# An mLSTM block with two MLPs on one core: the first block's weight split is moved beside the second block's tiles, its units run two at a time, and the gates' weights take 8 passes

## The reference

```python
h_in = rmsnorm(x, norm1_w)
q, k, v, o_pre = h_in @ wq, h_in @ wk, h_in @ wv, h_in @ w_og     # 8 heads
i_pre, f_pre = softcap(h_in @ w_ig + b_ig), softcap(h_in @ w_fg + b_fg)
Fcum = cumsum(log_sigmoid(f_pre))
Dmat = Fcum[:, None] - Fcum[None, :] + i_pre[None, :]; m = max(causal(Dmat))
C = (q @ k.T / sqrt(dqk)) * exp(Dmat - m)
h = (C / max(abs(sum(C)), exp(-m))) @ v
x1 = x + (sigmoid(o_pre) * headnorm(h)) @ w_out
h2 = rmsnorm(x1, norm2_w)
block = x1 + silu(h2 @ w_gate) * (h2 @ w_up) @ w_down              # FF = 2048
ghost = silu(x @ lut[gate_idx].T) * (x @ lut[up_idx].T) @ lut[down_idx].T   # 1376 inner
```

## Time and profile before

| | us |
|---|---|
| median of 3 runs | 2609.22 (2608.56 to 2611.22) |
| the profiled execution, its own time | 2609.44 |
| its span, first to last instruction | 2607.3 |

### The profile page before, as it was taken

The page is one execution under the profiler, slowest core; times in us unless marked ns, Lnnn a source line. Parts: engine busy times, 40 slices in busy tenths (PEclk is TensorE's granted clock), DMA queues, the critical chain, the costliest instruction groups (busy, mean ns, idle before and its releaser), DMA issues. The chain is left out here.

```text
span 2607.3 us, 32285 instructions
## 1 busy us (share of the span) xinstructions
PE 2458.7 (94%) x11024; PEld 1986.6 (76%) x11024; DVE 1270.9 (49%) x2185; ACT 914.5 (35%) x1667; POOL 605.7 (23%) x498
## 2 busy tenths in 40 slices
PE   6565999999999999999999999989999999999998
PEld 5344787877777777787777777768888888888887
DVE  5552563577477467557746746754322222222222
ACT  5313212444445353544444535346211111111111
POOL 4532221222122122222213212222111111111111
PEclk9568999999999999999999999999999999999999
DMA  5534645246445544724644554476687678767865
GB/s 219 205 142 148 243 154 198 98 157 234 158 148 190 205 144 161 290 96 159 230 161 143 198 202 145 160 285 224 220 288 272 242 261 290 256 239 278 284 213 199
DMA packets 117333, 530.32 MB, mean 203 GB/s; under 512 B 11280, under 2 KB 11280, under 8 KB 80304
## 3 DMA queue, kind: packets, MB, share of 16 engines
q1 hardware_dynamic: 110544, 515.86, 55.9%
q10 hardware_dynamic: 6624, 12.32, 1.6%
HBM read 440.46 MB, written 87.69 MB: 203 GB/s over the span
## 5 line engine op out<-in xcount | busy, mean ns | idle before, releaser
L1814 POOL TENSOR_TENSOR hidden_lo<-hm,hidden_hi 128x512 fp32r<-128x512 f32 x216 | 287.4, 1331 | 1360.7 <-ACT hidden_hi L972 1360.7
L664 PE MATMUL gate_bank<-act_hi,gud 128*128 128x512 f32 x1728 | 580.2, 397 | 17.1 <-DMA gud<-mlp_parts 9.0
L664 PE MATMUL up_bank<-act_hi,gud 128*128 128x512 f32 x1728 | 591.9, 404 | 0.0
L664 PE MATMUL acc<-gud,hidden_hi 128*128 128x512 f32 x1728 | 541.2, 395 | 16.8 <-POOL hidden_lo L1814 16.8
L1384 DVE SCALAR_TENSOR_TENSOR th<-th,gate_bank 128x512 f32<-128x512 f32 x216 | 147.9, 685 | 516.2 <-ACT th L967 516.2
L664 PEld LDWEIGHTS gate_bank<-act_hi,gud 128*128 128x128 f32 x1728 | 326.5, 189 | 85.4 <-issue 17.9
L664 PEld LDWEIGHTS up_bank<-act_hi,gud 128*128 128x128 f32 x1728 | 324.9, 188 | 79.2 <-issue 13.5
L664 PEld LDWEIGHTS acc<-gud,hidden_hi 128*128 128x128 f32 x1728 | 318.6, 188 | 83.4 <-issue 12.2
L972 ACT ACTIVATE hidden_hi<-hm 128x512 fp32r<-128x512 f32 x216 | 135.9, 629 | 697.9 <-PE acc L664 694.8
L664 PE MATMUL gate_bank<-act_lo,gud 128*128 128x512 f32 x864 | 338.2, 391 | 0.0
L664 PE MATMUL acc<-gud,hidden_lo 128*128 128x512 f32 x864 | 337.6, 391 | 0.0
(11 more groups left out here) (243 smaller groups left out, 3009.1 us busy)
## 6 DMA issues: line engine op xcount, KB each, us to landing
gud<-mlp_parts SPq DMA_DIRECT2D x128, 1024.0 KB, 5.1
gud<-ghost_parts SPq DMA_DIRECT2D x88, 1024.0 KB, 5.7
gud<-mlp_parts SPq DMA_DIRECT2D x128, 512.0 KB, 3.8
gud<-ghost_parts SPq DMA_DIRECT2D x88, 512.0 KB, 4.6
mlp_parts<-gud SPq DMA_DIRECT2D x16, 1536.0 KB, 6.0
ghost_parts<-look_w SPq DMA_DIRECT2D x35, 512.0 KB, 4.2
vo_w_hi<-vo_parts SPq DMA_DIRECT2D x12, 1024.0 KB, 5.9
vo_w_lo<-vo_parts SPq DMA_DIRECT2D x12, 1024.0 KB, 9.8
```

Source lines behind the costliest of these rows:

```text
L664: mm = pe.matmul(dst, l[a], r[c], start=first and k == 0 and n == 0, stop=last and k == len(lhs) - 1 and n == 2)
L1814: pool.tensor_tensor(HH[1][:], hm[:], HH[0][:].bitcast(f32), ALU.subtract).then_inc(of.low.sem, 1)
```

## The change

It does five things.

1. *Split.* Nothing of `mlp_parts` is made in FIRST. Tiles 0 and 1 are split in SECOND's front, tiles 2 to 15 in step t of `tiles(SECOND)`, gate and up parts in step t - 1, the down part in step t. PE uses the split tile from `gud` directly. A raw buffer of four tiles lies over the v/o weights, which are stored before and reloaded after (`reload_vo`, 4 MB). ACT's 128x1536 copy becomes one of 128x1024 and one of 128x512; POOL's three subtractions stay.
2. *Units.* FIRST's odd units get banks ACC[0], ACC[1] and buffers of their own. unit_1(u + 1) is put ahead of unit_2(u) on PE and DVE. x_T(FIRST), the second block's layer norm and the copy of its rows move into the units; the last ho_T, out-projections, x1 and h2 of FIRST move into SECOND's front.
3. *Gates.* High and low gate weights stand side by side as 32 columns: 8 passes instead of 12; two small DVE operations add the two halves.
4. *Block end.* x_T uses four banks, x_T(0) to x_T(3) all stand ahead of down(14), and down(15) moves behind the next front's gates. The wait for `mlp_rows` moves from DVE's first step of the front to ACT's row copy and to DVE's `cum`.
5. *Smaller moves.* In step 10 product(10) comes ahead of h2_scale(2). In TAIL the first index load is issued before the tiles, and bit_0 follows product(0) instead of preceding gated(0).

The core of the diff follows: the step counter, then SP, PE, ACT and DVE.

```diff
+class FirstAhead(Steps):
+    def of(self, at, k, name):
+        if not isinstance(at[0], int) or at != (0, 0):
+            return Steps.of(self, at, k, name)
+        i, n, e = self.names.index(name), len(self.names), self.early
+        if i < e:
+            return self.credit + i + 1 + (e + (k - 1) * n if k else 0)
+        return self.credit + e + k * n + (e if k + 1 < self.per_pass else 0) + i - e + 1
...
+        def xt_bank(at, i):
+            return AB[i % 2] if here(at, PRE) else ACC[2 + i % 2] if here(at, FIRST) else (B, A, GB, UB)[i]
...
-            load_mlp(0)
-            load_mlp(1)
...
-            for m in range(1, NM):
-                store_mlp(m)
-            for z in range(2):
-                sp.wait_ge(st_parts[z], 16 * (NM // 2))
-            load_gu(MLP, FIRST, 0)
+            store_vo(2)
+            wait(sp, vec_ln, FIRST, 0, f"xn{NB - 1}")
+            load_mlp(0)
+            wait(sp, vec_xT, FIRST, NB - 1, "lo")
+            store_xt(1, XH[1])
+            wait(sp, vec_x1, FIRST, NB - 1, "x1")
+            sp.dma_start(rows_of(x1_rows, 0), XN[0][:]).then_inc(st_x1, 16)
+            sp.wait_ge(mlp_lo[1], 1)
+            load_mlp(1)
+            sp.wait_ge(st_vo, 64)
+            wait(sp, pe_o, SECOND, NB - 1)
+            for m in (2, 3, 4):
+                load_mlp(m)
...
+                    if here(at, SECOND):
+                        store_gu(t)
+                        if t:
+                            store_dn(t - 1)
+                        if 2 <= t and t + 3 < NM:
+                            load_mlp(t + 3)
...
+                if here(at, SECOND):
+                    store_dn(NM - 1)
+                    reload_vo(1)
+                    reload_vo(2)
+                    for z in range(2):
+                        sp.wait_ge(st_gu[z], 16 * NM // 2)
+                        sp.wait_ge(st_dn[z], 16 * NM // 2)
+                    load_gu(MLP, at, 0)
...
+                if of is MLP and here(at, FIRST):
+                    pe.wait_ge(mlp_lo[0], t + 1)
+                else:
+                    pe.wait_ge(ld_gu[z], loads(of, at, t))
...
-                split(UB[0:2 * H, :], [pair(WG, S_, k, S_) for k in range(KT)],
-                      [pair(XH[at[1]], S_, k, S_) for k in range(KT)]).then_inc(pe_gates.sem, 1)
+                for k in range(KT):
+                    pe.matmul(UB[0:4 * H, :], WG[:, k, :, :], XH[at[1]][0][:, k, :], start=k == 0, stop=False)
+                    mm = pe.matmul(UB[0:2 * H, :], WG[:, k, 0, :], XH[at[1]][1][:, k, :], start=False, stop=k == KT - 1)
+                mm.then_inc(pe_gates.sem, 1)
+                if not isinstance(at[0], int):
+                    down(MLP, previous(previous(at)), NM - 1, NM - 1)
...
                 proj(at, 1)
+                if here(at, SECOND):
+                    ho_T(FIRST, NB - 1)
                 q_k_T(at, 0)
+                proj(at, 2)
                 if here(at, SECOND):
                     for i in range(NB):
-                        h2_T(FIRST, i)
-                proj(at, 2)
+                        out_proj(FIRST, i)
...
+            unit_1(FIRST, 0)
             for u in range(UNITS):
-                unit_1(FIRST, u)
+                if u + 1 < UNITS:
+                    unit_1(FIRST, u + 1)
                 unit_2(FIRST, u)
                 unit_3(FIRST, u)
-                if u in (2, 4, 6):
+                if u in (3, 5, 7):
                     ho_T(FIRST, u // 2 - 1)
+                if u in (4, 5):
+                    for i in (0, 1):
+                        x_T(FIRST, 2 * (u - 4) + i, xn_first)
...
+                    if t:
+                        hid(MLP, mb, t - 1)
+                        if here(at, SECOND) and t >= 2:
+                            mlp_hi_(t, 1)
+                    tanh(MLP, mb, t, stage)
                     if stage and t < UNITS:
-                        unit(t)
+                        unit(at, t)
+                    if here(at, SECOND) and 1 <= t < NM - 1:
+                        mlp_hi_(t + 1, 0)
...
+                unit_1(at, 0)
+                for u in range(UNITS):
+                    if u + 1 < UNITS:
+                        unit_1(at, u + 1)
+                    weights(at, u)
+                    if u in (2, 4, 6):
+                        norm_1(at, u // 2 - 1)
+                    if u in (3, 5, 7):
+                        norm_2(at, u // 2 - 1)
+                    unit_2(at, u)
+                    unit_3(at, u)
+                    if u == 1:
+                        ln_stats(at, x_raw, 1, 16)
+                    if u == 3:
+                        ln_apply(at, xn_first, 1, x_raw)
```

More of the change, by code:

```diff
@@ L551, in tiles @@
                 stored = span_of(kind)[0]
-                if not here(at, TAIL):
+                if not here(at, TAIL) and not here(at, SECOND):
                     wait(sp, vec_xT, mb, NB - 1, "lo")
@@ L563, in tiles @@
                         load_gu(MLP, at, 0)
-                    load_dn(MLP, mb, t)
+                    if not here(at, SECOND):
+                        load_dn(MLP, mb, t)
                     if looks(at):
@@ L751, in ho_T @@
                 wait(pe, vec_norm, at, i, "gated")
-                wait(pe, vec_unit, at, min(2 * i + 2, UNITS - 1), "heads")
+                if not here(at, FIRST):
+                    wait(pe, vec_unit, at, min(2 * i + 2, UNITS - 1), "heads")
+                elif i and i < NB - 1:
+                    wait(pe, vec_hoT, at, i - 1, "lo")
                 f = hn[:, :, :].rearrange("p h d -> p (h d)")
-                transposes(A, [f[:, k * P:(k + 1) * P] for k in range(KT)], pe_hoT)
+                transposes(ho_bank(at, i), [f[:, k * P:(k + 1) * P] for k in range(KT)], pe_hoT)
             def out_proj(at, i):
@@ L862, in front @@
                     proj(at, n)
+                    if n == 6 and here(at, SECOND):
+                        for i in range(NB):
+                            h2_T(FIRST, i)
                 wait(pe, act_gates, at, 0, "exps")
@@ L1072, in front, with split @@
                 first = here(at, FIRST)
-                def split(n):
-                    if first:
-                        mlp_hi_(n)
-                    elif here(at, SECOND):
-                        mlp_hi_(NM - 4 + n)
+                def split(m):
+                    if here(at, SECOND):
+                        for part in (0, 1):
+                            mlp_hi_(m, part)
                 def h2_T(i):
@@ L1124, in front @@
                 if looks(at) and half == 0:
-                    act.wait_ge(mlp_lo, NM)
                     load_idx(at, 0)
+                if here(at, SECOND):
+                    wait(act, vec_norm, FIRST, NB - 2, "sums")
                 logits()
@@ L1131, in front @@
                 qk(1)
+                if here(at, SECOND):
+                    ho_T(FIRST, NB - 1)
                 qkT_(0)
-                if here(at, SECOND):
-                    for i in range(NB):
-                        h2_T(i)
                 wait(act, vec_rows, at, 0, "biased")
@@ L1149, in front @@
                     act.wait_ge(vec_w, 3 * KT)
+                elif here(at, SECOND):
+                    act.wait_ge(st_x1, 16)
+                    wait(act, vec_h2, FIRST, NB - 1)
+                else:
+                    act.wait_ge(st_mlp[1 - half], b * 16)
                 act.activation(sp_, UB[32:40, :], ACT.Copy).then_inc(act_gates.sem, 1)
-                split(1)
                 qkT_(2)
@@ L1665, in tiles @@
                         look_up(at, steps_taken(look_kind(at), t))
[L1666 removed]
+                    if stage:
                         if t == 11:
@@ L1709, in _ @@
             looked = 0
-            for z in range(2):
-                dve.wait_ge(ld_vo[z], 32 + 32 * HALVES * (BATCH - 1))
-            bit_0(TAIL, 0)
             tiles(TAIL)
@@ L1879, in tiles @@
+                        if here(at, SECOND) and t >= 2:
+                            mlp_lo_(t, 1)
                         if t in (9, 10):
@@ L1888, in tiles @@
                             done += 1
-                    if stage and not first:
+                    if stage:
                         if t == 12:
@@ L1893, in tiles @@
                             ln_root1(at, 1 - half)
-                if first:
-                    for i in range(NB):
-                        x1_root(at, i)
-                    return
                 hid(MLP, mb, NM - 1)
-            tiles(FIRST)
+            units_first()
             tiles(SECOND)
```

674 lines of the change are left out of this document (360 added, 314 removed).

## The result

The changed kernel takes 2531.23 us (median of 4 runs, 2529.34 to 2532.11) against 2610.22 for the kernel before in the same comparison: a ratio of 0.9697, 95% interval 0.968 to 0.9713. It is faster, by 79 us where 89 were forecast, and inside the range. The profiled execution took 2532.11 us, its span is 2530.2; the span of before was 2607.3, so the two traces differ by 77.1 us.

What follows compares the result with a forecast made beforehand. PE was taken to bound the kernel from 437 us on, serial chains before the first MLP tile; 73 + 1.9 - 2 + 10.6 - 2.5 + 8.1 = 89.1 off 2609.4 gave 2520 us, range 2503 to 2547.

Steps and rivals of the forecast that it cites:

- FIRST's front: Start of FIRST: four gate passes and four splits go, so the first scores come at 68.3 instead of 71.70 us.
- FIRST's units: Unit stretch of FIRST: overlapped units, added up by DVE's work, let SECOND's gates start at 132 us instead of 184.7.
- 159 us as the time without it: SECOND's gates if in-order DVE keeps a unit at 11.6 us: start 159, kernel 2547; a rival given 6%.
- SECOND's front: Before the first MLP gate: 52 us of PE plus 5 of waits, gate at 189 instead of 262.3, 73 us less.
- the two new waits: SECOND's front: about 1.5 us for q_k_T(3) and about 2.3 for v(3) on ACT, taken as 5 in all.
- SECOND's tiles: SECOND's 16 MLP tiles: 1.9 us less for the first gate's clock, 2 us charged for the split beside them.
- The first rival: SECOND's eight unit steps: POOL's subtractions block DVE and half reaches PE, 15 us, so 2535; chance 14%.
- The bound of 48 subtractions: SECOND's tiles: upper bound of the split's charge, 48 subtractions of 1.27 us, 61 us.
- Block ends: Six block ends: gates lose 0.92 us, down(15)'s wait loses 0.85, together 10.6 us less.
- the eight gate passes cover 1.85: Block ends: gates ahead of down(15) cover 1.85 of its 2.3 us for the low part, leaving 0.45 of 1.3.
- TAIL: TAIL's start: index load issued before the tiles removes the stall of 8.2 us and more, 8.1 us less net.
- so nothing: Block end before TAIL: no gates cover down(15)'s wait for the low part, so no gain was counted there.

Runs made afterwards that it cites:

- Run 6: The changed kernel with FIRST's units one at a time again, on PE and VectorE: 2539.13 us, 7.9 more than the changed kernel.
- runs 9 and 10: The kernel before with GpSimd's low parts of weight tiles 2 to 15 cut to 8 columns, then ScalarE's high parts too: 2590.18 and 2581.69 us.
- run 7: The changed kernel with GpSimd's low-part subtractions for MLP weight tiles 2 to 15 cut from 512 to 8 columns: 2522.10 us, 9.1 less.
- run 8: The changed kernel with product(10) on VectorE behind all h2 work of its step again: 2526.38 us, 4.9 less by the medians.
- run 3: The changed kernel with PE's three loop passes written out, the other engines keeping their loops: 2522.51 us, 8.7 less.
- Run 4: The changed kernel with down(15) back at the end of the block's tiles, ahead of the next block's gates: 2547.74 us, 16.5 more.
- Run 11: The changed kernel with PE's loop written out, the fourth root first, product(10) late, TAIL's tile loads early and SyncE's waits behind TAIL's tiles: 2509.08 us.
- run 2: The changed kernel with GpSimd taking the fourth x1 root ahead of the weight subtractions in SECOND's step 10: 2526.11 us, 5.1 less.

## Why the prediction was right, and where it was not

**FIRST's front.** First scores at 66.9, for 68.3: as said, a little more.

**FIRST's units.** SECOND's gates at 135.2, for 132 with bounds of 127 and 137. The terms as they stand add up to 134.7, (70.4 + 48 + 4 + 12.3), so the 132 is wrong by its own terms, and so are the bounds, which come to 129 and 140. The sum by VectorE held: 46.3 us busy for 48. Its idle time was larger, 22.6 us for 16, as the clock in the stretch is 0.65 and not halfway to full. Where the 44 us from scores(0) to the gates came from, I had wrong. I put nearly all on the overlap and gave 159 us as the time without it. Run 6 says 144.5. The 44.3 us, (112.64 - 68.30), part like this. 6.7 go to the splits that left (runs 9 and 10), of which the prediction had 5. 24.4 are the work between the last unit and SECOND's gates (in the kernel before, the last `kv` ends at 159.9 and the gates start at 184.3), which moved under other work or into the front. 9.2 are the pairs (run 6; up to 13 by the fastest of the nine traces). The 4.1 left are what the new order of norms, layer norm and transposes gives beyond what it took in; no run takes that out alone.

**SECOND's front.** 54 us for 57; the two new waits cost less than the 5 taken. The first gate at 189.59, for 189: **72.7** for 73.

**SECOND's tiles.** This step failed. Taking from 174.7 us the down(15) that moved out, 2.8, its wait of 1.25 and the 1.9 for the gate's clock, 168.8 would have been left, and run 7, where the low parts of the split are left out and its high parts and DMAs stay, gives 168.6. The changed kernel has 176.3: the split costs 7.5, where I charged 2. The clause at fault is "Each step gets ... POOL three subtractions": I weighed them against the low part of the tile and not against the roots in the same queue. That was 4.8; the two engines standing in each other's way, 2.9. The first rival's mechanism is there at a fifth of its price. (The bound of 48 subtractions counts tiles 0 and 1, which are split in the front: 42 stand beside the tiles.)

**Block ends.** Where no edge follows, a block is 2.70 us shorter (217.03 to 214.33), for a net 1.35. By terms: down(15)'s wait is 0.39 (0.45 said), the gates 0.94 (0.92), down(10) costs 0.34 (0.42; run 8). Of the other 1.2 to 1.3, 0.95 lie in unit step 4 of every looped block, gate(4) to gate(5): 12.63 to 12.67 us before, 11.66 to 11.70 after. They come from a move that neither the list of changes nor the prediction names: in the even unit steps GpSimd now takes the norm's root ahead of the tile's low part, not behind it. Before, the low part stood beside VectorE's square of the heads, which took 1.67 us, and PE waited for what follows:

```profile
519.87 1.39 POOL L1814 TENSOR_TENSOR hidden_lo<-hm,hidden_hi 128x512 fp32r<-128x512 f32 x1 [4.09 <-ACT hidden_hi L972]
520.14 1.67 DVE L1586 TENSOR_TENSOR ar<-hn 128x512 f32<-128x512 f32 x1
523.22 1.12 PE L729 MATMUL bank_b<-qbd,qkT 128*128 128x512 f32 x2 [0.73 <-DVE tt L1562]
```

After, the square takes 0.69 us, the root starts at 453.10 and the low part behind it:

```profile
451.40 0.69 DVE L1689 TENSOR_TENSOR ar<-hn 128x512 f32<-128x512 f32 x1
454.70 1.30 POOL L1942 TENSOR_TENSOR hidden_lo<-hm,hidden_hi 128x512 fp32r<-128x512 f32 x1
```

The traces show both sides of it; no run undoes this move alone.

Where the back edge follows, a block gains only 1.05 and 0.42 us (218.20 to 217.15, 217.66 to 217.24), and the one behind it 1.65. The step "the eight gate passes cover 1.85" is true for four of the six ends only, since in the other two the jump now stands bare between down(14) and the gates. The two jumps cost 7.9 us in this trace against blocks without one (run 3), where the kernel before had paid 1.8 (218.20 and 217.66 against 217.03), with 1.2 and 0.7 us idle at the jump for 2.7 and 2.7 now. Why it paid less stays open. Run 4 puts down(15) back ahead of the jump and the idle time stays 5.4 in all, so that it hid beside that wait isn't the explanation.

So the sum of the block ends comes near its forecast by luck: some 5.7 us won by GpSimd's order and some 6 more lost at the jumps cancel, and the prediction had neither.

**TAIL.** This step failed too: 8.1 forecast, 1.2 measured (866.6 us from the first gate to the span's end before, 865.4 after). "Issued before the tiles it has landed by then" was right for the index. What I didn't ask is what is late next, and it was the second gate tile, 6.1 us, hidden until then behind the stall. Run 11 shows the step's size: 858.6, so 8.0 less than before once that tile is early, and down(0) then waits 1.76 for its low part, for the 1.8 that I had named. Before TAIL, down(15) waits 2.21 us instead of 1.25, as nothing covers it: "so nothing" was 0.9 too kind.

**The sum.** Behind the first gate 16.1 were forecast and 4.4 came. SECOND's tiles lack 5.5 and TAIL 6.9. The six block ends gave 8.8 for 8.1: 7.5 in the five periods, and the rest in the last block and at SECOND's end, as the ends without an edge gave more than forecast and those with one less. 16.1 - 5.5 - 6.9 + 0.7 = 4.4.

## To carry to other kernels

Where a stall is removed, list the transfers and queued instructions whose lateness it hid, with the time each is issued: the next wait is among them. Where work is put on a queue that has time to spare, look for the short instruction behind it that others wait for; here 3.7 us of subtractions cost nothing by their sum, and 4.8 by one root behind them. A product that is pulled out from between others as cover must be checked at the loop's jump too, where the cover isn't there; writing one engine's three passes out was worth 7.9 us by the periods and 8.7 by the medians. A diff has more in it than the list of what was meant: compare the engines' orders step by step, as one swap on GpSimd gave 0.95 us in each looped block.

## What was not expected of the hardware

- The jump back of PE's loop leaves PE idle, with no releaser: 2.7 us both times in the changed kernel, 1.9 to 3.6 over all eight traces of the changed kernel and the runs on it that keep the loop, and 0.7 to 1.2 in the kernel before and runs 9 and 10. The matmuls behind it can run at 1.2 GHz for a while: 797.5 to 801.5 us has a granted clock of 0.57. Behind 7 of the 16 jumps they don't, and the length of the idle time doesn't decide it (half clock behind 1.9 us in run 4, full clock behind 3.3 in run 6). Without the jump (runs 3 and 11) there is neither.
- The same holds for waits. One of 3.1 us, in SECOND's step 10, was followed by a granted clock of 0.66 over 5 us in five traces and of 1.00 in two. One of 2.21 us, at a block's end in run 4, was followed by half clock in four of the six blocks. Of the 3.2 us between the blocks of 219.4 and 216.2, 1.6 is that and 1.6 stands behind the jump. So the cover of one such wait is worth 2.75 us on the mean (16.5 / 6), not 1.85. So one trace of such a kernel can be 1.6 us off at each place of this kind.
- What a GpSimd subtraction does to VectorE depends on the operands. With the root first (run 2), VectorE's operations stand beside 4.42 us of three subtractions:

```profile
311.50 4.42 POOL L1927 TENSOR_TENSOR gud<-raw_mlp,gud 128x512 fp32r<-128x512 f32 x3 [1.36 <-ACT gud L1080]
311.51 0.68 DVE L1514 TENSOR_TENSOR qbd<-bank_b,n 128x512 f32<-128x512 f32 x1
312.11 0.97 DVE L1504 TENSOR_SCALAR ex<-xn,rs 128x512 f32<-128x512 f32 x1
313.00 0.68 DVE L1514 TENSOR_TENSOR ct<-bank_a,n 128x512 f32<-128x512 f32 x1
313.60 1.17 DVE L1520 TENSOR_TENSOR act_lo<-qbd,act_hi 128x512 fp32r<-128x512 f32 x1
314.70 1.77 DVE L1520 TENSOR_TENSOR act_lo<-ct,act_hi 128x512 fp32r<-128x512 f32 x1
```

  Those that read a bank keep their 0.68 us; those with both inputs in SBUF take 1.17 and 1.77. In run 7, without the subtractions, the latter take 0.68 and 0.69. The product by one number per row, `ex`, takes 0.97, and 0.49 in run 7, though it reads one large tile only. The Trainium skill says so too, Advanced Engine Details and Errata, section "GPSIMD Details": GpSimd conflicts with VectorE's instructions that have two SBUF inputs or run in a 2-port performance mode. The trace agrees on the first; no row tells in which mode `ex` ran. Read ahead, it would have told that the units' `ct` and `ar`, which read a bank, are safe and the norm's two products are not.
